# Values' products directly behind k's, scores behind them, and the waits of both at k's last product

## The chip, the core and the metric

The kernel runs on one core of one Trainium2 chip. The core has five engines with a queue of instructions each: TensorE (PE in the profile, with its weight loads shown apart as PEld), VectorE (DVE), ScalarE (ACT), GpSimd (POOL) and SyncE (SP), which here issues the DMAs. Each takes its instructions in the order in which they are written, and they meet at semaphores. The metric is the device time of one execution in microseconds; lower is better.

## What is computed

An input of 128 images with 224 channels and 32 x 32 positions is normalized by groups (16 stripes of two columns), then goes through attention, and is added to the result:

```
xh = group_norm(x)
q, k, v = xh @ Wq, xh @ Wk, xh @ Wv             # 224 -> 224, 8 heads of 28
sim  = q * scale @ k^T + pos_emb                # per head: 16 windows against 16 windows
attn = softmax(sim)                             # for each of 64 places within a window
o    = attn @ v
out  = x + (o @ Wo + bo)
```

The attention is small: each of the 64 places in an 8 x 8 window attends over the same place of the 16 windows, so a score block is 16 x 16 for every head and place.

## The kernel before, in words

An image has 1024 tokens. The work is cut into 512 steps of 256 tokens (two tiles of 128), four steps to an image and two to a half of an image. Every engine runs a function `step(t, i)` for t in order; the middle 480 steps are a loop of 24 steps a round. A step does the stages of different steps of the pipeline: in TensorE's step t the projections belong to u = t + 4, the scores to t + 1, the values' products to t - 2 and the output projection to t - 3.

TensorE's step t, in order (L376 to L424):

- q's product of u (6 matmuls of 512 columns into `ps_q`), v's (12 of 224 columns into `ps_v`), k's (6 of 512 columns into `ps_k`). Before the last of k's six stands `score_waits()` (L379): the scores of t + 1 wait there for `biased` of step t (VectorE has read the scores of step t out of their only buffer, `ps_s`), and in every second step for the block-diagonal keys `k_bd` and for q.
- the scores of t + 1 (`score`, L349): 32 small products of 64 rows and 32 columns, each half of the 128 rows into its own half of `ps_s`; the last raises `scored`.
- three waits, and the values' products of t - 2 (`weigh_values`, L364): 16 small products of 128 rows and 32 columns into `ps_o`; the last raises `pv_done`. They wait for the probabilities `p_bd`, placed by four DMAs, for v in SBUF, and for `o_lo` of t - 3: VectorE has read `ps_o`.
- the output projection of t - 3 into `ps_out` (12 matmuls), behind waits for `o_lo` and `final`; once in four steps a product that totals the squares of an image (`ps_tot`).

The other engines around it:

- ScalarE (step L490) copies q (L501), v (L507), takes the exponential (L511), normalizes x (L484, four instructions a step), copies k into `k_cut` (L518), adds a bias (L470, in two of four steps), and copies the values' result out of `ps_o` into `ohi` (L526). Every second step it also makes `xhi`, the upper 16-bit part of the normalized x (L495). The copy of k waits for `k_done` and for `scored`, because `k_cut` and `k_bd` have two buffers: for even u, the scores asked for are those of t + 1, the ones that TensorE issues right behind this k; for odd u those of t.
- VectorE (step L638) begins with `olo` (L646: what `ohi` lost of `ps_o`), then reads the scores (L651), takes their maximum (L658), transposes the probabilities of the step before (L664), adds the output (L634), and sums (L676).
- GpSimd (step L719) subtracts the maximum (L724), makes `xlo` (L732) in every second step, and multiplies by the reciprocal (L737). The two parts `xhi` and `xlo` are what TensorE's next q product with an even u waits for (L390).

Of the kernel before, what the change touches and what calls it, by code (L numbers as in the profile page):

```python
# [49 lines left out]
PV_LAG, OUT_LAG, FINAL_LAG, STORE_LAG = 2, 3, 4, 7  # L50
# [8 lines left out]
def build(nc, x, wq, wk, wv, wo, bo, pos, scale, out):  # L59
    ctx = ExitStack()  # L60
    with ctx:
# [6 lines left out]
        def sem(name):  # L68
            return ctx.enter_context(nc.semaphore(name))
# [92 lines left out]
        k_done = sem("k_done")  # L162
# [3 lines left out]
        v_kept = sem("v_kept")  # L166
# [11 lines left out]
        pv_done = sem("pv_done")  # L178
        o_hi = sem("o_hi")
        o_lo = sem("o_lo")  # L180
# [7 lines left out]
        def wait(eng, s, n, i, per_round):  # L188

            if isinstance(i, int):  # L190
                if n > 0:
                    eng.wait_ge(s, n)
            else:
                assert n > 0
                eng.wait_ge(s, n + i * per_round)
# [13 lines left out]
        def per_step(eng, s, g, i, each=1):  # L209
            wait(eng, s, each * (g + 1), i, each * PERIOD)  # L210

        def per_half(eng, s, h, i, each=1):
            wait(eng, s, each * (h + 1), i, each * PERIOD // 2)

        def per_image(eng, s, b, i, each=1):
            wait(eng, s, each * (b + 1), i, each * PERIOD // 4)

        def keys_placed(eng, h, i):
            each = 16 * HPG
            wait(eng, k_placed[h % 2], each * (h // 2 + 1), i, each * PERIOD // 4)  # L220

        def probs_placed(eng, g, i):
            each = 16 * PAIRS
            wait(eng, p_placed[g % 2], each * (g // 2 + 1), i, each * PERIOD // 2)

        def image_at(t, lead):
            b, r = divmod(t + lead, 4)
            return b if r == 0 and 0 <= b < B else None
# [5 lines left out]
        def is_step(g):  # L234
            return 0 <= g < STEPS
# [83 lines left out]
        def _(pe):  # L319
            def split_product(dst, w_parts, x_parts, chunks=CH, waits=None):  # L320

                n = 0
                for a, c in PASSES:
                    for ch in range(chunks):
                        if waits is not None and n == 3 * chunks - 1:
                            waits()
                        last = nc.tensor.matmul(dst, w_parts(a, ch), x_parts(c, ch),  # L327
                                                start=(n == 0), stop=(n == 3 * chunks - 1))
                        n += 1
                return last  # L330
# [4 lines left out]
            def project_qk(u, j, waits=None):  # L335
                h, hg = divmod(u, 2)
                c0 = (j * HG + hg) * 128
                return split_product(ps_qk[j][:, :], lambda a, ch: wqk[:, a, ch, c0:c0 + 128],
                                     lambda c, ch: x_parts[c][:, h % 2, ch, :], CH, waits)

            def project_v(g):
                for t2 in range(T2):
                    tok = ((g % 2) * T2 + t2) * TILE
                    last = split_product(ps_v[:, t2, 0:C],
                                         lambda a, ch: x_parts[a][:, (g // 2) % 2, ch, tok:tok + TILE],
                                         lambda c, ch: wv_s[:, c, ch, :])
                return last
# [16 lines left out]
            def weigh_values(g):  # L364
                for t2 in range(T2):
                    for hg in range(HG):
                        for h in range(HPG):
                            unit = (((h // 2) * T2 + t2) * HG + hg) * 2 + h % 2
                            col = (t2 * HG + hg) * 128
                            last = nc.tensor.matmul(  # L370
                                ps_o[h * 32:h * 32 + 32, col:col + 128].rearrange("p (r j) -> p r j", j=32),
                                v_sb[:, g % VBUFS, t2, hg * HPG + h, :],
                                p_bd[:, g % 2, :, unit * 32:unit * 32 + 32], start=True, stop=True)
                return last

            def step(t, i):  # L376
                u = t + PROJ_LEAD

                def score_waits():  # L379
                    g = t + 1  # L380
                    if is_step(g):
                        if g % 2 == 0:
                            keys_placed(pe, g // 2, i)
                            per_step(pe, q_kept, g + 1, i)

                        per_step(pe, biased, g - 1, i)

                if is_step(u):
                    if u % 2 == 0:
                        per_half(pe, x_hi, u // 2, i)  # L390
                        per_half(pe, x_lo, u // 2, i)
                    per_step(pe, q_kept, u - 1, i)
                    project_qk(u, 0).then_inc(q_done, 1)
                    per_step(pe, v_kept, u - 1, i)
                    project_v(u).then_inc(v_done, 1)
                    per_step(pe, k_kept, u - 1, i)
                    project_qk(u, 1, score_waits).then_inc(k_done, 1)
                else:
                    score_waits()
                if is_step(t + 1):  # L400
                    score(t + 1).then_inc(scored, 1)
                g = t - PV_LAG
                if is_step(g):
                    probs_placed(pe, g, i)
                    per_step(pe, v_kept, g, i)

                    per_step(pe, o_lo, g - 1, i)
                    weigh_values(g).then_inc(pv_done, 1)
                g = t - OUT_LAG
                if is_step(g):  # L410
                    per_step(pe, o_lo, g, i)
                    per_step(pe, final, g - 1, i)
                    for ch in range(CH):
                        last = split_product(
                            ps_out[0:CP, ch * 256:ch * 256 + 256].rearrange("p (nh t y) -> p nh t y", nh=NW, t=T2),
                            lambda a, hg: wo_s[:, a, hg, ch * CP:(ch + 1) * CP],
                            lambda c, hg: o_parts[c][:, g % 2, hg::HG].rearrange("p t (nh nw) c -> p nh t (nw c)", nh=NW), HG)
                    last.then_inc(projected, 1)
                b = image_at(t, TOT_LEAD)
                if b is not None:  # L420
                    per_image(pe, joined, b, i)
                    wait(pe, stats, STAT_OPS * (b - 1) + 1, i, STAT_OPS * XBUFS)
                    nc.tensor.matmul(ps_tot[0:CP, :], ones[0:CP, 0:CP], both[:, b % 2],  # L423
                                     start=True, stop=True).then_inc(totals, 1)  # L424
# [342 lines left out]
```

## Time and profile before

| | |
|---|---|
| median of 3 runs | 3675.77 us (3672.93 to 3676.39) |
| the profiled execution's own time | 3674.84 us |
| its span, first to last instruction | 3672.9 us |
| PE busy | 3608.4 us (98% of the span) |
| PEld, DVE, ACT, POOL busy | 71%, 83%, 80%, 56% |
| values' products (L370) and scores (L358), mean of one | 276 ns and 224 ns |
| granted TensorE clock | 1.00 in the whole span (the 2.4 GHz level) |
| PE's share of the chain that ended last | 87% |

PE is the engine that has almost no idle time; the others wait, for each other and for PE. A matmul's end is modelled and overlaps the start of the next, so distances between stages are read from start to start. The profile's rows join equal neighbours ("x2"); the start is that of the first.

### The profile page before, as it was taken

Reading aid. Unit: us, or ns where it says so; the run is one execution under the profiler, and the core shown is the slowest. Engines: PE = TensorE matmul, PEld = TensorE weight load, DVE = VectorE, ACT = ScalarE, POOL = GpSimd, SP = SyncE. Lnnn points to the kernel's source line nnn. Section 1 sums busy time; section 2 is a strip of 40 time slices with the busy share of each in tenths; the row PEclk is TensorE's granted clock in tenths of the full one; section 3 lists DMA queues with packets and bytes.
Section 4 is the critical chain, followed back from the end, with each engine's and each line's share of the span. In section 5 each row is a group of like instructions: output and inputs, shape, how many; then the busy total and the mean of one; then the engine's idle time right before and its main releaser. Section 6 shows DMA issues by size and latency. Waiting matters only on the chain.

```text
span 3672.9 us, 167555 instructions
## 1 busy us (share of the span) xinstructions
PE 3608.4 (98%) x67842; PEld 2625.2 (71%) x67842; DVE 3032.9 (83%) x5028; ACT 2940.0 (80%) x5377; POOL 2045.4 (56%) x3334
## 2 busy tenths in 40 slices
PE   5999999999999999999999999999999999999998
PEld 3777777777777777777777777777777777777776
DVE  6888888888888888888888888888888888888876
ACT  6888888888888888888888888888888888888874
POOL 4555555555555555555555555555555555555553
PEclk9999999999999999999999999999999999999999
DMA  4555555555555555555555555555555555555544
GB/s 95 139 144 136 146 144 142 137 145 143 141 138 150 142 137 143 145 143 137 143 146 144 136 145 144 144 134 145 143 145 135 145 142 145 136 146 143 141 126 117
DMA packets 252111, 513.67 MB, mean 140 GB/s; under 512 B 62672, under 2 KB 63120, under 8 KB 251536
## 3 DMA queue, kind: packets, MB, share of 16 engines
q1 hardware_dynamic: 250000, 504.35, 52.4%
q8 instruction: 554, 9.08, 1.1%
q10 hardware_dynamic: 1536, 0.07, 0.0%
q14 instruction: 21, 0.17, 0.0%
HBM read 118.31 MB, written 117.44 MB: 64 GB/s over the span
## 4 chain that ended last, share of the span: by engine, by line
PE 87%; issue 5%; POOL 3%; DVE 2%; ACT 1%; DMA 0%; POOLq 0%; SPq 0%; DVEq 0%; ACTq 0%
PE ps_out L327 18%; PE ps_q L327 16%; PE ps_k L327 16%; PE ps_v L327 14%; PE ps_o L370 13%; PE ps_s L358 10%; POOL sc L724 1%; ACT xn L484 1%; POOL xlo L732 1%; POOL newton L706 1%; DVE part L622 0%; POOL sc L737 0%; PE ps_tot L423 0%; DVE sc L651 0%; DVE pt_f L664 0%
## 5 line engine op out<-in xcount | busy, mean ns | idle before, releaser
L724 POOL TENSOR_TENSOR sc<-sc,mx 128x512 f32<-128x512 f32 x512 | 536.5, 1048 | 876.3 <-DVE mx L658 876.3
L484 ACT ACTIVATE xn<-x_sb,norm_add,norm_mul 112x128 f32<-112x128 f32 x2048 | 1016.7, 599 | 5.0 <-POOL norm_add L717 3.1
L737 POOL TENSOR_TENSOR sc<-sc,rs 128x512 f32<-128x512 f32 x512 | 536.4, 1048 | 421.7 <-DVE rs L678 421.6
L327 PE MATMUL ps_out<-ohi,wo_s 128*112 128x256 f16 x4096 | 720.8, 278 | 3.1 <-DVE x_sb L634 3.1
L646 DVE TENSOR_TENSOR olo<-ps_o,ohi 128x512 f16<-128x512 f32 x512 | 353.8, 691 | 350.0 <-ACT ohi L526 338.8
L511 ACT ACTIVATE sc<-sc 128x512 f32<-128x512 f32 x512 | 323.3, 632 | 396.3 <-POOL sc L724 396.1
L327 PE MATMUL ps_q<-xhi,wqk 112*128 112x512 f16 x2048 | 611.2, 380 | 12.5 <-POOL xlo L732 9.9
L327 PE MATMUL ps_k<-xhi,wqk 112*128 112x512 f16 x2048 | 609.7, 379 | 0.6 <-ACT q_sb L501 0.6
L370 PE MATMUL ps_o<-p_bd,v_sb 128*32 128x128 f32 x16384 | 553.5, 276 | 9.1 <-DMA p_bd<-pt_f 6.6
L327 PE MATMUL ps_v<-wv_s,xhi 112*128 112x224 f16 x4096 | 560.6, 259 | 0.0
L732 POOL TENSOR_TENSOR xlo<-xn,xhi 112x1024 f16<-112x1024 f32 x256 | 547.3, 2138 | 13.1 <-ACT xhi L495 13.1
L327 PEld LDWEIGHTS ps_out<-ohi,wo_s 128*112 128x112 f16 x4096 | 447.6, 129 | 104.8 <-issue 103.7
L358 PEld LDWEIGHTS ps_s<-k_bd,q_sb 64*32 64x32 f32 x32768 | 360.7, 105 | 218.3 <-issue 215.0
L327 PEld LDWEIGHTS ps_v<-wv_s,xhi 112*128 112x128 f16 x4096 | 395.9, 98 | 121.4 <-issue 0.6
L370 PEld LDWEIGHTS ps_o<-p_bd,v_sb 128*32 128x32 f32 x16384 | 417.3, 109 | 58.4 <-DMA p_bd<-pt_f 7.5
L358 PE MATMUL ps_s<-k_bd,q_sb 64*32 64x64 f32 x32768 | 443.3, 224 | 2.6 <-DVE sc L651 2.6
L501 ACT ACTIVATE q_sb<-ps_q 128x512 f32<-128x512 f32 x512 | 300.4, 587 | 166.0 <-PE ps_q L327 165.0
L327 PE MATMUL ps_out<-olo,wo_s 128*112 128x256 f16 x2048 | 391.1, 273 | 0.0
L651 DVE SCALAR_TENSOR_TENSOR sc<-ps_s,s_scale,pos_sb 128x512 f32<-128x512 f32 x512 | 379.6, 741 | 0.0
L507 ACT ACTIVATE v_sb<-ps_v 128x448 f32<-128x448 f32 x512 | 274.6, 536 | 122.3 <-PE ps_v L327 121.1
L634 DVE SCALAR_TENSOR_TENSOR x_sb<-ps_out,out_scale,x_sb 112x512 f32<-112x512 f32 x512 | 366.5, 716 | 3.3 <-PE ps_out L327 1.7
L327 PE MATMUL ps_v<-wv_s,xlo 112*128 112x224 f16 x2048 | 364.0, 259 | 0.0
(76 smaller groups left out, 5827.6 us busy)
## 6 DMA issues: line engine op xcount, KB each, us to landing
k_bd<-k_cut SPq DMA_DIRECT2D x1024, 128.0 KB
p_bd<-pt_f SPq DMA_DIRECT2D x2048, 64.0 KB, 2.5
x_sb<-in_x SPq DMA_DIRECT2D x256, 448.0 KB, 4.5
out_y<-x_sb SPq DMA_DIRECT2D x256, 448.0 KB, 3.5
k_cut<-in_L_conv_Wq SPq DMA_DIRECT2D x2, 98.0 KB
k_cut<-in_L_conv_Wk SPq DMA_DIRECT2D x2, 98.0 KB
k_cut<-in_L_conv_Wv SPq DMA_DIRECT2D x2, 98.0 KB
pt_f<-in_L_conv_Wo SPq DMA_DIRECT2D x8, 24.5 KB
```

The lines of the kernel that those rows point to most:

```text
L327: last = nc.tensor.matmul(dst, w_parts(a, ch), x_parts(c, ch), start=(n == 0), stop=(n == 3 * chunks - 1))
L358: last = nc.tensor.matmul(ps_s[pr * 32:pr * 32 + 32, half, col:col + 64].rearrange("p (h j) -> p h j", j=32), q_sb[rows, h % QBUFS, hg, to ...
L370: last = nc.tensor.matmul(ps_o[h * 32:h * 32 + 32, col:col + 128].rearrange("p (r j) -> p r j", j=32), v_sb[:, g % VBUFS, t2, hg * HPG + h ...
L484: nc.scalar.activation(xn[:, b % 2, :, c4, :, :, nw].rearrange("p r c q -> p q r c"), x_sb[:, b % XBUFS].rearrange("p ch (nh r w) -> p (ch ...
L501: nc.scalar.activation(q_sb[:, h % QBUFS, hg], ps_qk[0][:, :], ACT.Copy).then_inc(q_kept, 1)
L511: nc.scalar.activation(sc[:, t % 2], sc[:, t % 2], ACT.Exp).then_inc(exped, 1)
L634: nc.vector.scalar_tensor_tensor(xr, ps_out[0:CP, :].rearrange("p (q y) -> p q y", q=CH * NW), out_scale[0:CP, :], xr, ALU.mult, ALU.add). ...
L646: nc.vector.tensor_tensor(olo[:, g % 2], in_x_order(ps_o[:, :]), ohi[:, g % 2], ALU.subtract).then_inc(o_lo, 1)
L651: nc.vector.scalar_tensor_tensor(sc[:, t % 2].rearrange("p (a c) -> p a c", a=2), ps_s[:, :, 0:256], s_scale[:, :], pos_sb[:].rearrange("p ...
L724: nc.gpsimd.tensor_tensor(rows, rows, mx[:, t % 2].unsqueeze(2).broadcast_to(by_row), ALU.subtract).then_inc(shifted, 1)
L732: nc.gpsimd.tensor_tensor(by_channel_half(xlo[:, h % 2]), half_of_xn(h), by_channel_half(xhi[:, h % 2]), ALU.subtract).then_inc(x_lo, 1)
L737: nc.gpsimd.tensor_tensor(rows, rows, rs[:, t % 2].unsqueeze(2).broadcast_to(by_row), ALU.mult).then_inc(probs, 1)
```

## The change

The waits of the values' products go into the same function as those of the scores, ahead of k's last product, and the values' products are issued directly behind k's, with the scores behind them. The scores are cut into halves of 64 rows before as after; `score` and `weigh_values` are the same. No other engine's instructions change.

```diff
-                def score_waits():
+                def attention_waits():
+                    g = t - PV_LAG
+                    if is_step(g):
+                        probs_placed(pe, g, i)
+                        per_step(pe, v_kept, g, i)
+
+                        per_step(pe, o_lo, g - 1, i)
                     g = t + 1
                     if is_step(g):
                         if g % 2 == 0:
...
                     per_step(pe, k_kept, u - 1, i)
-                    project_qk(u, 1, score_waits).then_inc(k_done, 1)
+                    project_qk(u, 1, attention_waits).then_inc(k_done, 1)
                 else:
-                    score_waits()
+                    attention_waits()
+                if is_step(t - PV_LAG):
+                    weigh_values(t - PV_LAG).then_inc(pv_done, 1)
                 if is_step(t + 1):
                     score(t + 1).then_inc(scored, 1)
-                g = t - PV_LAG
-                if is_step(g):
-                    probs_placed(pe, g, i)
-                    per_step(pe, v_kept, g, i)
-
-                    per_step(pe, o_lo, g - 1, i)
-                    weigh_values(g).then_inc(pv_done, 1)
                 g = t - OUT_LAG
```

On PE, in a step of the loop with an even u, before (`ps_s` are the scores, `ps_o` the values' products, `p_placed0` the probabilities, `biased` the read of the scores before):

```order
L327 MATMUL ps_k<-xhi,wqk 128x512
L327 MATMUL ps_k<-xhi,wqk 128x512 [waits biased]
L358 MATMUL ps_s<-k_bd,q_sb 32x64 x32
L195 REGISTER_ALU
L370 MATMUL ps_o<-p_bd,v_sb 32x128 [waits o_lo,v_kept,p_placed0]
L370 MATMUL ps_o<-p_bd,v_sb 32x128 x15
L327 MATMUL ps_out<-ohi,wo_s 112x256 [waits final,o_lo]
```

The same place in the changed kernel:

```order
L327 MATMUL ps_k<-xhi,wqk 128x512
L195 REGISTER_ALU
L327 MATMUL ps_k<-xhi,wqk 128x512 [waits o_lo,biased,v_kept,p_placed0]
L370 MATMUL ps_o<-p_bd,v_sb 32x128 x16
L358 MATMUL ps_s<-k_bd,q_sb 32x64 x32
L327 MATMUL ps_out<-ohi,wo_s 112x256 [waits final,o_lo]
```

The 16 values' products have moved ahead of the 32 scores, and their three waits with the register instruction to k's last product.

On ACT, the end of a step in which the bias is added, and the start of the next; these rows are the same before and after:

```order
L518 ACTIVATE k_cut<-ps_k 128x512 [waits scored,k_done]
L484 ACTIVATE xn<-x_sb,norm_add,norm_mul 112x8x8x2 x2
L195 REGISTER_ALU [waits normed]
L470 ACTIVATE x_sb<-x_sb,bo_sb 112x1024 [waits summed]
L526 ACTIVATE ohi<-ps_o 128x512 [waits projected,pv_done]
L495 ACTIVATE xhi<-xn 112x1024 [waits k_done,normed]
L501 ACTIVATE q_sb<-ps_q 128x512 [waits scored,q_done]
```

Nothing moves here. The `scored` that `k_cut` waits for is raised by the last of the scores, which in the changed kernel stand behind the values' products.

## Rows read from the trace of the kernel before

**Rows 1.** Waits between 100 and 3500 us: engine line <- engine line: us, times, longest
```profile
POOL sc L724 <- DVE mx L658: 817.4, 483, 3.3
DVE olo L646 <- ACT ohi L526: 304.4, 363, 1.2
```
**Rows 2.** One line in that window, DVE L651: instances, min/median/max ns, first and last start
```profile
L651 DVE SCALAR_TENSOR_TENSOR sc<-ps_s,s_scale,pos_sb x483: 740/741/745, 101.3 to 3494.5; 128x512 f32<-128x512 f32 x161
```
**Rows 3.** Timeline of PE, steps A to D: start, us, engine, line, op, count
```profile
3243.25 0.59 PE L327 MATMUL ps_k<-xhi,wqk 112*128 112x512 f16 x2
3243.78 0.86 PE L358 MATMUL ps_s<-k_bd,q_sb 64*32 64x64 f32 x64
3244.57 1.08 PE L370 MATMUL ps_o<-p_bd,v_sb 128*32 128x128 f32 x32
3245.58 0.43 PE L327 MATMUL ps_out<-ohi,wo_s 128*112 128x256 f16 x2
...
3254.05 0.60 PE L327 MATMUL ps_q<-xhi,wqk 112*128 112x512 f16 x2
3254.48 0.59 PE L327 MATMUL ps_q<-xlo,wqk 112*128 112x512 f16 x2
...
3268.10 0.60 PE L327 MATMUL ps_q<-xhi,wqk 112*128 112x512 f16 x2
...
3271.41 0.59 PE L327 MATMUL ps_k<-xhi,wqk 112*128 112x512 f16 x2
```
**Rows 4.** Timeline of ACT in the same stretch
```profile
3244.85 0.66 ACT L518 ACTIVATE k_cut<-ps_k 128x512 f32<-128x512 f32 x1
...
3259.94 0.62 ACT L518 ACTIVATE k_cut<-ps_k 128x512 f32<-128x512 f32 x1
```
**Rows 5.** Timeline of DVE in the same stretch
```profile
3247.83 0.69 DVE L646 TENSOR_TENSOR olo<-ps_o,ohi 128x512 f16<-128x512 f32 x1 [0.28 <-ACT ohi L526]
```
**Rows 6.** Timeline of POOL in the same stretch
```profile
3249.97 1.05 POOL L724 TENSOR_TENSOR sc<-sc,mx 128x512 f32<-128x512 f32 x1 [3.23 <-DVE mx L658]
3250.98 2.14 POOL L732 TENSOR_TENSOR xlo<-xn,xhi 112x1024 f16<-112x1024 f32 x1
...
3265.05 2.14 POOL L732 TENSOR_TENSOR xlo<-xn,xhi 112x1024 f16<-112x1024 f32 x1
```
**Rows 7.** Timeline of all engines near 3626 us, where k_cut waits for the scores
```profile
3625.98 0.86 PE L358 MATMUL ps_s<-k_bd,q_sb 64*32 64x64 f32 x64
...
3626.94 0.60 ACT L518 ACTIVATE k_cut<-ps_k 128x512 f32<-128x512 f32 x1 [1.08 <-PE ps_s L358]
```
**Rows 8.** Timeline near 140 us, where q follows xlo closely
```profile
138.41 2.13 POOL L732 TENSOR_TENSOR xlo<-xn,xhi 112x1024 f16<-112x1024 f32 x1
...
140.46 0.38 PE L327 MATMUL ps_out<-ohi,wo_s 128*112 128x256 f16 x2
...
140.77 0.60 PE L327 MATMUL ps_q<-xhi,wqk 112*128 112x512 f16 x2
```
**Rows 9.** Timeline of another such stretch, 228 to 257 us
```profile
228.42 0.59 PE L327 MATMUL ps_k<-xhi,wqk 112*128 112x512 f16 x2
...
230.64 0.63 ACT L518 ACTIVATE k_cut<-ps_k 128x512 f32<-128x512 f32 x1
...
250.78 2.13 POOL L732 TENSOR_TENSOR xlo<-xn,xhi 112x1024 f16<-112x1024 f32 x1
...
253.19 0.60 PE L327 MATMUL ps_q<-xhi,wqk 112*128 112x512 f16 x2
...
256.50 0.59 PE L327 MATMUL ps_k<-xhi,wqk 112*128 112x512 f16 x2
```
**Rows 10.** What the values' products (L370) waited for, whole span: us, times
```profile
issue: 6.9, 31
```
**Rows 11.** SP's timeline after 3249 us, and p_bd's DMAs: KB each, median us to landing
```profile
3250.63 2.43 SPq L302 DMA_DIRECT2D p_bd<-pt_f  x4
...
p_bd<-pt_f SPq DMA_DIRECT2D x1932, 64.0 KB, 2.5
```

## The prediction

> **What bounds the kernel now.** I read the page's busy times first. PE is busy in 98% of the span and 87% of the last chain is PE, so it sets the time. Then the waits: POOL waits 817 us for VectorE's maximum, VectorE 304 us for ACT's `ohi`, in a window of 3400 us [rows 1]; ACT's exponential in turn takes what POOL made. So the softmax engines are not full, but each waits for the next of them: they form a ring, and a delay put into it anywhere goes round. A step takes (3494.5 - 101.3) / 482 = 7.04 us, four steps 28.16 us [rows 2]. The pattern repeats every four steps; I call them A to D, A being the one that ends with `ps_tot`. I look at one such stretch from 3243 us on [rows 3 to 6], and at one near 228 us. In the second, PE needs 256.50 - 228.42 = 28.08 us for four steps [rows 9]: I take that for PE running freely; the mean is 0.08 us over it.
>
> **PE's own part: nothing.** From the start of k's last pair to the scores it takes 0.53 us, from the scores' start to the values' 0.79, from the values' to the output projection 1.01, together 2.33 us [rows 3]. In the new order the same pieces stand as 0.53 (k's pair), 1.01 (values), 0.79 (scores), again 2.33. I take it that a distance belongs to the product in front: its streaming and the emptying of the array behind it. What the change of neighbours could do is bounded by the rows too. A pair of 512-column products takes 0.43 us where the next is of its kind (3254.05 to 3254.48), and 0.53 before the scores: the emptying costs 0.10. So 0.10 us a step is what a cheaper neighbour could give, and as much I allow for a dearer one. I take zero, since the values and the output projection both use 128 rows and their distance is not shorter for it.
>
> The Trainium skill (TensorEngine Tiling (Array Packing), Key Properties) says that changing the tiling mode drains TensorE. There are three changes of mode in a step before and three after, so by that rule the sum is zero as well; if only a change of the row split drained, the step would lose one drain, 0.10 us. The row from the values to the output projection speaks for the rule.
>
> **The waits that move.** The values' three waits and their register instruction stand between scores and values now, and cost PE 6.9 us in 31 places in the whole run [rows 10]. Behind k's fifth product they are covered by the products still queued there. None comes later than the wait for `biased`, which is there already: `olo` of that step ends at 3247.83 + 0.69 = 3248.52, and VectorE writes it just before it reads the scores. The probabilities' four DMAs are issued from 3250.63 to 3253.06 and land some 2.5 us later, at about 3255.6 [rows 11]; the values that need them follow the k of the next step, step C's at 3257.36. That leaves 1.8 us. In front of the output projection stand two waits, `o_lo` and `final`, now behind the scores; the values' own three, which stood there, fit into that distance in all but those 31 places. So the gain is at most 6.9 us, and only if PE sets the time everywhere.
>
> **What the later scores do.** This is the term that decides. The scores now start at 3243.25 + 0.53 + 1.01 = 3244.79 and end 0.86 later at 3245.65, where before they ended at 3244.64 [rows 3]. Their users:
>
> - VectorE's read of them (L651) stands behind `olo`, which ends at 3248.52 [rows 5], 2.9 us after the new end; no cost.
> - `k_cut` of an even u asks for just these scores. Where it waited for them, it started 3626.94 - (3625.98 + 0.86) = 0.10 us behind their end [rows 7]. So in step A it can start at 3245.75 at the earliest. It starts at 3244.85 now [rows 4]: it is held 0.90 us. In step C it starts at 3259.94 [rows 4]; k's last pair began at 3254.05 + 3.31 = 3257.36 (the 3.31 is worked out below), so it is 2.58 us behind k already, and the new bound is 2.50: no new wait; B and D ask for scores of the step before.
>
> Behind `k_cut` in ACT's queue stand normalization, bias and `ohi`, and nothing of it can pass. The Trainium skill says the same of ScalarE's queue (TensorE: Matmul & The Clock Gate, the table at its head: a strict FIFO of 8); by a queue that let `ohi` pass, the whole term below would be zero.
>
> From there I follow the ring in the rows: `k_cut` 3244.85 [rows 4], `olo` 3247.83, waiting for `ohi` [rows 5], the maximum, then POOL's L724 at 3249.97 after 3.23 us of idleness for the maximum, and `xlo` right behind it, 3250.98 to 3253.12 [rows 6]. Nobody in this chain has a pause in which 0.90 us could vanish: VectorE waits for ACT, POOL for VectorE, `xlo` stands behind POOL's L724. So `xlo` ends at 3254.02. PE's q of step C starts at 3254.05 [rows 3]. The slack of 0.93 us is used up.
>
> How close may q follow `xlo`? Near 140 us, `xlo` ended at 140.54 and q started at 140.77, 0.23 us behind, and 0.31 after the last pair of the output projection instead of 0.22 (the pace of such pairs): there the wait was felt [rows 8]. In the code the semaphore wait, a register instruction with the second wait, and a third wait on q's first product follow each other. So q of C moves to 3254.25, by 0.20.
>
> The delay goes on in the ring: `k_cut` of C follows that of A by 15.09 us (3259.94), the next `xlo` starts at 3265.05 and ends at 3267.19 [rows 6], 22.34 us after A's `k_cut`. With the 0.90 it ends at 3268.09, and q, at 3268.10 before [rows 3], starts 0.23 later at 3268.32. Again 0.22 late, the first 0.20 included. Then A comes again, and again `k_cut` waits for the scores: the ring is tied to PE there, and PE to the ring at q, so the delay repeats every four steps.
>
> The new cycle, from k's last pair in A to the next: 0.53 + 1.01 + 0.86 + 0.10 = 2.50 to `k_cut`; 22.34 to the end of `xlo`; 0.23 to q; 3271.41 - 3268.10 = 3.31 to k's last pair: 28.38 us. In the stretch of rows 9, where the ring already runs later relative to PE, the middle is 250.78 + 2.13 - 230.64 = 22.27 and the cycle 2.50 + 22.27 + 0.23 + 3.31 = 28.31. I take their mean, 28.34. Against 28.16 that is 0.18 us per four steps; 483 steps are 120.75 cycles [rows 2], so +21.7 us. The ends of the run I leave out. The 6.9 us do not come back, as PE waits for `xlo` anyway.
>
> 3674.84 + 21.7 = 3696.6 us by the profiled execution. Its time is 0.9 us under the median of the runs, so I say 3697.
>
> **Bounds.** The 0.23 could be as short as the handing over of 0.10 that `k_cut` showed: the cycle is then 28.21 and the loss 6 us, 3681. At the other end, the full 28.38 and no relief: +0.22 x 120.75 = 27 us, 3702, and some us more where the probabilities, whose slack falls from 1.8 to 0.9 us, come late in a step with more DMAs.
>
> **Rivals.**
>
> 1. The ring has cover. Somewhere the 0.90 us is caught (a wait that I took for a link is slack) and `xlo` stays ahead of q. Then only the waits' gain is left, 6.9 us or less: 3668 to 3676. For it: 0.93 us of slack at q is just as much as the hold of 0.90, and PE before has a slack everywhere. Against: q needs 0.23 us more than the bare end of `xlo`. Chance 0.10, half of it inside 0.2%.
> 2. Cheaper changes of mode: k's products and the values' both use all rows, so the values start without a drain, 0.10 us x 512 steps = 51 us: 3624. Against: the same pair of row splits stands between values and output projection now and is no shorter. 0.03.
> 3. The wait for the probabilities decides, now ahead of k's last product. The place is k of step C, with B's probabilities; it binds from 1.8 us of added delay on [rows 11], and earlier where DMAs of x and of the output stand in front in SP's queue. The ring's 0.9 brings it half way. If it cost 0.20 us, as the wait at q does, once in four steps on top, that is 128 x 0.20 = 26 us: 3723. Chance 0.06.
> 4. The ring is held, but q can follow closely: loss 3 to 8 us, 3678 to 3683. 0.10, a third of it inside 0.2%.
>
> My forecast has 0.71. About 0.2% (7 us) is what a measurement of this kernel tells from no change. Slower: 0.71 + 0.06 + 0.07 = 0.84. Same: 0.05 + 0.03 = 0.08. Faster: 0.05 + 0.03 = 0.08. The range reaches from 3678 to 3708.
>
> **What would show it.** In the profile after: PE's distances k to values 0.53, values to scores 1.01, scores to output 0.79; ACT's `k_cut` waiting for `ps_s` about 120 times, some 0.6 to 0.9 us each, where the waits before have no such row; `q` starting about 0.23 us behind the end of `xlo`, with an idle of PE before it put down to POOL L732, about 240 times; the slack of `biased` at k's last product down to a few tenths. I am wrong if q of steps A and C still follows the output projection at 0.22 us, or if `k_cut` shows no wait for the scores.

## The result, and the profile after

The changed kernel takes 3719.29 us (median of 6 runs, 3709.58 to 3723.88), the kernel before 3675.31 us beside it (6 runs, 3672.93 to 3676.39): ratio 1.0117, 95% interval 1.0105 to 1.0129, a loss of 44 us. I had forecast a loss of 22, with 3708 as the high end. The direction and its mechanism came out as forecast; the size did not. The profiled execution of the kernel after took 3719.29 us, with a span of 3717.5.

The page's head of the kernel after, with the busy times:

```profile
span 3717.5 us, 167883 instructions
PE 3641.3 (98%) x67842; PEld 2614.5 (70%) x67842; DVE 3033.2 (82%) x5028; ACT 2924.8 (79%) x5377; POOL 2044.2 (55%) x3334
```

PE's busy time grew by 33 us with the same products (short waits vanish under the modelled ends, and products at the lower clock count longer), so the page's shares tell nothing here. DVE and POOL worked as long as before, ACT 15 us less. The waits between 100 and 3500 us, as in [rows 1]: engine and line that waited, what for, us, times, longest:

```profile
POOL sc L725 <- DVE mx L659: 842.6, 477, 5.1
ACT sc L512 <- POOL sc L725: 506.3, 469, 1.4
DVE olo L647 <- ACT ohi L527: 396.7, 382, 1.7
...
PEld ps_q L327 <- issue: 35.9, 149, 0.6
PEld ps_k L327 <- issue: 23.8, 96, 0.4
PEld ps_out L327 <- issue: 12.4, 22, 2.6
ACT k_cut L519 <- PE ps_s L358: 10.5, 31, 1.3
PE ps_out L327 <- issue: 8.5, 5, 2.4
```

Two rows of the kernel before, for comparison:

```profile
ACT sc L511 <- POOL sc L724: 364.8, 483, 1.4
...
PEld ps_q L327 <- issue: 2.1, 5, 0.6
```

Three things to see. The ring waits longer at every link: VectorE for `ohi` 397 us instead of 304, ACT for POOL 506 instead of 365. The weight loads of q wait 149 times, about 0.24 us each; before, 5 times. And there is a row that nothing in my forecast spoke of: PE standing in front of the output projection, 5 times, up to 2.4 us.

One cycle of four steps in the kernel after, the rows that answer to [rows 3, 4, 6]. Timeline of PE, ACT and POOL: start, us, engine, line, what:

```profile
3223.62 0.59 PE L327 MATMUL ps_k<-xhi,wqk 112*128 112x512 f16 x2
3224.14 1.08 PE L370 MATMUL ps_o<-p_bd,v_sb 128*32 128x128 f32 x32
3225.15 0.91 PE L358 MATMUL ps_s<-k_bd,q_sb 64*32 64x64 f32 x64
3225.99 0.43 PE L327 MATMUL ps_out<-ohi,wo_s 128*112 128x256 f16 x2
...
3226.09 0.60 ACT L519 ACTIVATE k_cut<-ps_k 128x512 f32<-128x512 f32 x1 [0.26 <-PE ps_s L358]
...
3232.17 2.12 POOL L733 TENSOR_TENSOR xlo<-xn,xhi 112x1024 f16<-112x1024 f32 x1
...
3234.53 0.60 PE L327 MATMUL ps_q<-xhi,wqk 112*128 112x512 f16 x2
...
3246.20 2.13 POOL L733 TENSOR_TENSOR xlo<-xn,xhi 112x1024 f16<-112x1024 f32 x1
...
3248.57 0.60 PE L327 MATMUL ps_q<-xhi,wqk 112*128 112x512 f16 x2
...
3251.88 0.59 PE L327 MATMUL ps_k<-xhi,wqk 112*128 112x512 f16 x2
```

k to values 0.52, values to scores 1.01, scores to output projection 0.84 (0.79 in most steps). `k_cut` begins 2.47 us behind k's last pair (2.50 forecast). From `k_cut` to the end of the next `xlo` it takes 3234.29 - 3226.09 = 8.20 us (8.27 in the rows before), and q starts 0.24 us behind the end of `xlo` in both places. The cycle is 3251.88 - 3223.62 = 28.26 us (28.34 forecast). This one is among the short ones: over the 119 cycles from one `ps_tot` to the next in the 480 steps counted below, the median is 28.34 us (28.14 before), just the forecast; the mean is 28.48 us (28.18 before), and what lies between median and mean is the unforeseen part.

The unforeseen part, in the kernel after. Timeline of PE near 1410 us; the figure in brackets is PE's idle time before the row and what ended it, "issue" being nothing that the profile shows:

```profile
1409.20 1.08 PE L370 MATMUL ps_o<-p_bd,v_sb 128*32 128x128 f32 x32
1410.21 0.86 PE L358 MATMUL ps_s<-k_bd,q_sb 64*32 64x64 f32 x64
1413.09 0.43 PE L327 MATMUL ps_out<-ohi,wo_s 128*112 128x256 f16 x2 [2.02 <-issue]
...
1414.46 1.06 PE L327 MATMUL ps_q<-xhi,wqk 112*128 112x512 f16 x2
```

And its stretches: us of the stretch, busy times, granted clock, DMA share:

```profile
1410.00:1414.00 4.00, 1.98 (x84) 1.62 (x76) 2.77 (x6) 3.43 (x8) 3.45 (x12) 1.00 0.38 102
1414.00:1418.00 4.00, 4.00 (x19) 2.19 (x17) 3.97 (x6) 1.50 (x3) 2.38 (x4) 0.57 0.15 35
```

PE stands still for 2.0 us, though what it waits for by the program (`o_lo`, `final`) is long there, and then works some 3.4 us at the 1.2 GHz level: the pair of q takes 1.06 instead of 0.60 us. One such event costs some 2.0 + 1.7 = 3.7 us.

### The profile page after: what moved, and what is told of

Read it like the earlier page. It is cut to its first block, busy times and chain, and to the rows that moved or that the text cites. A ratio compares the mean times of both kernels' runs of the same rounds, so it can differ in the third digit from the quotient of the medians.

```text
span 3717.5 us, 167883 instructions
## 1 busy us (share of the span) xinstructions
PE 3641.3 (98%) x67842; PEld 2614.5 (70%) x67842; DVE 3033.2 (82%) x5028; ACT 2924.8 (79%) x5377; POOL 2044.2 (55%) x3334
## 4 chain that ended last, share of the span: by engine, by line
PE 96%; issue 2%; DVE 1%; ACT 1%; SPq 0%; DMA 0%; POOL 0%; ACTq 0%; POOLq 0%; DVEq 0%
PE ps_out L327 20%; PE ps_q L327 18%; PE ps_k L327 17%; PE ps_v L327 16%; PE ps_o L370 14%; PE ps_s L358 11%; PE ps_tot L424 0%; DMA p_bd<-pt_f 0%; SPq L302 0%; ACT xn L485 0%; SPq L310 0%; DMA x_sb<-in_x 0%; DVE sc L652 0%; POOL xlo L733 0%; DVE pt_f L665 0%
## 5 line engine op out<-in xcount | busy, mean ns | idle before, releaser
L370 PEld LDWEIGHTS ps_o<-p_bd,v_sb 128*32 128x32 f32 x16384 | 417.1, 110 | 212.0 <-issue 201.5
L370 PE MATMUL ps_o<-p_bd,v_sb 128*32 128x128 f32 x16384 | 555.2, 276 | 9.2 <-DMA p_bd<-pt_f 9.1
L659 DVE TENSOR_REDUCE mx<-sc 128x16 f32<-128x512 f32 x512 | 351.3, 686 | 13.2
```

What stands on the lines that cost most here:

```text
L370: last = nc.tensor.matmul(ps_o[h * 32:h * 32 + 32, col:col + 128].rearrange("p (r j) -> p r j", j=32), v_sb[:, g % VBUFS, t2, hg * HPG + h ...
L659: nc.vector.reduce_max(mx[:, t % 2], rows, axis=AX.X).then_inc(maxed, 1)
```

## The experiments

Sixteen kernels were run. Each is told with the ratio to the kernel before on the same chip. For the accounting I took from each trace the same 480 steps, from k's last product of step 16 to that of step 496, and three sums: what the distance from the output projection to q is over its usual 0.11 us, without stalls; the distances over 1 us between two products of PE ("stalls"); and the stretches at the 1.2 GHz level between 100 and 3500 us, each of which costs about half its length.

```
kernel                               time us   480 steps   at q     stalls       at 1.2 GHz
before                               3675      3381.0       1.7      0    -         0    -
after                                3719      3418.3      27.3      5   10.2       3   10.2
e1  after, k_cut without `scored`    3671      3379.9       0.1      1    1.4       0    -
e2  before, the same                 3673      3379.1       1.1      0    -         0    -
e3  new order only                   3739      3437.3      30.4     20   32.6       0    -
e4  moved waits only                 3680      3383.5       1.6      5    8.8       0    -
e5  e3, k_cut without `scored`       3673      3378.4       0.8      0    -         0    -
e6  new order in steps A only        3732      3433.1      25.6     14   25.3       4   13.7
e7  new order in B, C, D only        3674      3378.1       0.6      1    1.8       0    -
e9  after, bias behind ohi           3670      3376.8       0.0      1    1.3       0    -
e8  e1 and e9 together               3673      3381.1       0.1      1    1.1       0    -
e11 before, bias behind ohi          3669      3377.5       0.1      0    -         0    -
e13 before, 128 waits at the head    3733      3434.7       0.1     19   47.7       7   23.9
e12 e5, the same                     3749      3456.4       0.1     20   58.4      13   44.4
e14 after, the same                  3814      3517.5      22.4     35   88.2      17   64.8
e10 e3, the same                     3830      3533.4      22.1     46  106.2      16   61.4
e15 after, 64 waits at the head      3811      3507.8      21.6     24   72.9      17   78.5
e16 after, 192 waits at the head     3779      3483.6      19.3     22   54.9      13   51.2
```

### Is it the wait of k_cut? (e1, e2)

e1 is the changed kernel, e2 the kernel before, both with this one line less (for even u it asks for the scores just issued):

```diff
                     per_step(act, k_done, u, i)
-                    per_step(act, scored, 2 * (h - 2) + 1, i)
```

> The changed kernel, but ScalarE's copy of k (k_cut) no longer waits for the scores; the buffer is still safe, since SyncE issues the DMAs out of k_cut only behind VectorE's transpose, which stands behind those scores. Theory H (the hold of k_cut by the later scores, carried round the ring of ScalarE, VectorE and GpSimd into xlo and from there into PE's q): k_cut in step A starts where it did before, 1.4 to 2.0 us behind k's last product, xlo is ahead of q again by 0.5 to 1 us, PE runs at 28.1 us per four steps, and the time is that of before or under it: 3660 to 3678. Theory W (PE's own order costs: the stalls of about 2 us in front of the output projection and the waits gathered at k's last product): the loss stays, 3705 to 3725, with xlo early. If H explains the regular part and the rare stalls are of the order itself, the time is 3678 to 3690 and the stalls in front of the output projection are still in the profile.

> The kernel before without the wait of k_cut for the scores, as a control for the run above. Before, k_cut waited for the scores hardly anywhere, so H and W both expect no change: 3670 to 3680. Were it faster by over 8 us, the wait itself (the two semaphores on one ScalarE instruction) would cost something, and the run above would have to be read against this one.

Measured: e1 3671.48 us (11 runs), ratio 0.9991 [0.9982, 1.0]; e2 3672.58, 0.9996 [0.9986, 1.0005]; both within what theory H expected. The whole 44 us is gone from the changed kernel with one wait of ACT, and the same wait is worth nothing in the kernel before. The order of the products therefore has no price of its own on PE, and in this pair, whose PE programs are the same, the stalls (1 instead of 5) and the slow stretches (none instead of 3) hang on the hold too.

### Which half of the change? (e3, e4)

e3 has the new order with the values' waits directly in front of the values (the diff is against the kernel before, where these lines stand behind the scores). e4 is the changed kernel with the two lines of the scores back in front of the two of the values: the moved waits and the old order.

```diff
+                if is_step(t - PV_LAG):                 # e3
+                    probs_placed(pe, t - PV_LAG, i)
+                    per_step(pe, v_kept, t - PV_LAG, i)
+                    per_step(pe, o_lo, t - PV_LAG - 1, i)
+                    weigh_values(t - PV_LAG).then_inc(pv_done, 1)
                 if is_step(t + 1):
                     score(t + 1).then_inc(scored, 1)
```

> Only the order of the change: values' products behind k and in front of the scores, but their three waits directly in front of them and not at k's last product. H expects what the changed kernel does, 3705 to 3725, with q 0.236 us behind xlo in steps A and C. W expects that the waits gathered at k's last product make up a good part of the loss, and so 3680 to 3700 here.

> Only the waits of the change: the values' three waits stand at k's last product, but the scores still come in front of the values' products. H expects no loss and at most the 6.9 us of issue gaps back: 3667 to 3677. W expects a loss of 10 us or more.

Measured: e3 3739.44 us, 1.0181 [1.0166, 1.0197]; e4 3680.46 us, 1.0018 [1.0009, 1.0027]. Theory H missed both: e3 is slower than its 3705 to 3725 us, e4 than its 3667 to 3677. So the order is what costs, and with it the moved waits help by 20 us; alone they cost 6. In e4 the gain that I had forecast did come: the distances from the scores to the values sum up to 70.1 us over the 480 steps, where the kernel before has 75.8. Five stalls of 8.8 us in all ate it. The waits of e3 between 100 and 3500 us:

```profile
PE ps_out L327 <- issue: 26.4, 19, 2.2
...
PE ps_q L327 <- issue: 6.9, 19, 0.7
```

In e3 a stall comes every 172 us, in 19 of the loop's 20 rounds, in front of the same output projection of the loop's body. In e4 four stand at that place and one at the loop's end, with no more loss at q than before, though 85 q products start within 0.4 us of the end of `xlo` (11 before, 221 in the changed kernel).

### Ring free, order kept (e5)

```diff
                     per_step(act, k_done, u, i)                   # in e3
-                    per_step(act, scored, 2 * (h - 2) + 1, i)
```

> The values' and scores' products in the new order, the values' waits directly in front of the values, and ACT's k_cut without its wait for the scores (a race-free cut here, since the scores that it waited for are read by VectorE before xlo can be reached). The run with the new order and the same places of the waits, but with k_cut's wait, took 3739 us and showed 19 stalls of 1.3 to 2.5 us on PE in front of or inside the output projection, once a round of the loop. Theory F (the stalls come when PE's sequencer has been let go late and has no lead over the engine; the held ring makes it late): the q waits go and the stalls mostly with them, 3672 to 3685 us, fewer than 8 rows of PE idle over 1 us in front of the output projection. Rival L (the stalls hang on where the instructions lie, whatever the ring does): only the q waits go (31 us of the 64), the 19 stalls stay, 3700 to 3712 us.

Measured: 3672.84 us, 0.9994 [0.9985, 1.0004], as theory F expected. All of e3's 64 us are gone. The row of its waits:

```profile
PE ps_out L327 <- issue: 0.6, 1, 0.6
```

The 19 stalls have gone with the hold of the ring, though PE's own program is the same, word for word. At this point I took the lateness of PE's sequencer (the part of PE that passes the waits and issues the instructions) for the whole cause of the stalls; the padded kernels below add a second sort.

### Which step? (e6, e7)

```diff
-                if is_step(t - PV_LAG):
+                values_first = t % 4 == 0       # e6; e7 has t % 4 != 0
+                if values_first and is_step(t - PV_LAG):
                     weigh_values(t - PV_LAG).then_inc(pv_done, 1)
                 if is_step(t + 1):
                     score(t + 1).then_inc(scored, 1)
+                if not values_first and is_step(t - PV_LAG):
+                    weigh_values(t - PV_LAG).then_inc(pv_done, 1)
```

> The changed kernel with the new order (values, then scores) only in the steps that I call A (every fourth), where k_cut asks for the scores just made; in the three others scores stand first again. All waits at k's last product. Theory H (the loss is the hold of k_cut in step A, carried round the ring): the loss stays whole, q about 0.24 us behind xlo in A and C, 3697 to 3720 us. Rival (the loss is made in every step, by the later scores or by the order of the modes): a quarter of 44 us, 3685 us or less.

> The complement: the new order in steps B, C and D, scores first in A. All waits at k's last product. Theory H: k_cut in A starts as early as in the kernel before (about 1.4 us behind k's last product began) and the loss is that of the moved waits alone, 3672 to 3684 us. Rival (the loss is made in every step): three quarters of 44 us, about 3708 us.

Measured: e6 3731.61 us, 1.016 [1.0133, 1.0187], above the 3720 us that theory H allowed; e7 3674.20 us, 0.9996 [0.9986, 1.0005], as it expected. The new order in one step of four makes the whole loss at q (25.6 us against 27.3); in the three others it makes none. e6 even came out 12 us above the changed kernel, all of it in stalls (14 against 5) and slow stretches: another arrangement of the same code, another number of stalls.

### Hold kept, ring shortened (e9)

```diff
-                add_bias(image_at(t, SPLIT_LEAD - 1), 0, i)
-                add_bias(image_at(t, SPLIT_LEAD - 2), 1, i)
...
                     nc.scalar.activation(ohi[:, g % 2], in_x_order(ps_o[:, :]), ACT.Copy).then_inc(o_hi, 1)
+                add_bias(image_at(t, SPLIT_LEAD - 1), 0, i)
+                add_bias(image_at(t, SPLIT_LEAD - 2), 1, i)
```

> The changed kernel with ACT's two add_bias moved from in front of ohi to behind it in the step, so that the ring from k_cut to xlo becomes about 1.0 us shorter in the step with the bias while k_cut is still held by the scores. Theory H (the loss is ring length, not the hold as such): k_cut of step A still starts 2.28 us behind k's last product, but xlo ends early enough again that q follows the output projection at its own pace; 3665 to 3682 us. Rival (the hold or the order costs PE by itself, or bias is late now and k's last product waits for it): 3700 us or more.

Measured: 3670.37 us, 0.9986 [0.9976, 0.9996]. Its waits between 100 and 3500 us:

```profile
DVE olo L647 <- ACT ohi L525: 294.8, 195, 2.6
...
ACT k_cut L519 <- PE ps_s L358: 179.9, 241, 1.1
ACT q_sb L502 <- PE ps_q L327: 179.5, 241, 1.4
```

`k_cut` is now held 241 times, 0.75 us each, 180 us in all: far more than in the changed kernel (31 times), and it costs nothing. This is the clearest of the runs: the hold is not the loss. The loss at q is a ring whose length, together with the hold, exceeds PE's four steps; with 1.1 us of bias out of its way it fits again. The Trainium skill (TensorE: Matmul & The Clock Gate, the table at its head) gives ScalarE's queue as strictly first in, first out. The trace agrees: `ohi` came earlier when it was put earlier in the queue, and VectorE waited 295 us for it instead of 397.

### A better kernel? (e8, e11)

e8 is e1 and e9 in one; e11 is the kernel before with only the bias moved.

> The changed kernel without k_cut's wait for the scores, and with ACT's add_bias behind ohi: both cuts of the ring at once, looked at as a candidate. Theory H (PE sets the time alone once the ring is free): like the two single cuts, 3665 to 3674 us, since PE's own 28.08 us per four steps, found in the stretch near 228 us, is the floor; no mid-run stretch at the 1.2 GHz level. Rival (the ring still costs something in the single cuts): 3660 us or less.

> The kernel before, with nothing changed but ACT's add_bias behind ohi. Theory H: the kernel before lost 0.08 us per four steps to the ring; without that 10 us less at most, 3665 to 3673 us. Rival (the gain of this edit needs the new order): 3673 us or more.

Measured, 11 runs each: e8 3673.09 us, 0.9995 [0.9986, 1.0004]; e11 3669.02 us, 0.9985 [0.9976, 0.9994]. Two cuts of the ring are no better than one: once the ring fits, PE alone sets the time. e11 is the fastest version found, by 0.15% (some 6 us), level with e9. The 1.7 us at q are gone, and its 480 steps take 3.5 us less; the new order adds nothing to it. The 28.08 us per four steps that the prediction took for PE running freely are its best case and not its mean: the cycles of e1, e2, e5, e7, e8, e9 and e11 average 28.13 to 28.17 us, against 28.18 in the kernel before. So the ring cost the kernel before a few microseconds at most, and not 0.08 us a cycle.

### Where the code lies (e10, e12 to e16)

The trace has a queue of the kind "instruction" (q8) with 554 transfers in the whole run, of about 1.1 us each; that they bring PE's instructions is borne out below, where more waits on PE alone make them more. At each of the four longest stalls of the changed kernel and of e3 (2.2 to 2.6 us from product to product), such a transfer begins between 0.12 us before and 0.35 us after the start of the last product in front of the stall. It holds for every stall of the table: in front of each of the 214 products that end one, the last transfer had ended 1.2 to 2.1 us before. A transfer comes every 6.6 us, so by chance this would be so for about one in seven. So I put more instructions at the head of PE's program, outside the loop, which moves the loop's code against the pieces in which it is delivered:

```diff
             pe.wait_ge(zeroed, N_ZEROED)
+            for _ in range(128):
+                pe.wait_ge(zeroed, N_ZEROED)
             rounds(pe, step, before_11=bound_weights, before_4=weights_split)
```

> The run with the new order and the values' waits directly in front of the values (3739 us, 19 stalls over 1.3 us of PE in front of the output projection, once a round of the loop at one place), with 128 more waits on a semaphore that has long been raised at the head of PE's program, outside the loop: the loop's instructions lie elsewhere. Theory F (the stalls are late deliveries of PE's instructions, which the trace shows as transfers of about 1 us): the stalls change their place or their number, the q waits (31 us) stay; 3705 to 3740 us. Rival S (the stalls are a late semaphore of another engine at that place of the schedule): they stay where they are, 19 of them, 3739 us within 4 us. If the loop's code keeps its place against the borders of the deliveries, F too would leave them there, and the run would not tell.

Measured: 3829.65 us, 1.0419 [1.0403, 1.0435], far above theory F's 3705 to 3740. 128 waits that are passed at once, outside the loop, cost 90 us. The page of e10, queue, packets, MB, share:

```profile
q8 instruction: 572, 9.37, 1.1%
```

18 more deliveries than the 554 of the kernels without padding, about one for each of the loop's 20 rounds. A late semaphore of another engine at one place of the schedule as the cause (rival S, 3739 us) is out.

> The new order with k_cut's wait taken away (3673 us), with the same 128 waits at the head of PE's program that took the version with the wait from 3739 to 3830 us. Theory F (a late delivery of instructions costs PE only where its sequencer has been let go late): the ring is free, so 3670 to 3690 us and few stalls over 1 us. Rival L (with this layout the deliveries are late whatever the ring does): about 90 us more than without the padding, 3740 us or more.

> The kernel before with the same 128 waits at the head of PE's program. Theory F: its q waits are passed with 0.5 to 1.0 us to spare, so some stalls at most: 3672 to 3700 us. Rival L: 90 us more, 3750 us or more. If it came out between, the lead of PE's sequencer in the kernel before would be just about what a delivery takes.

> The changed kernel with the same 128 waits. Theory F: its q waits (27 us) stay, and the stalls (12 us in the run, with their stretches at 1.2 GHz) come out in another number and at other places, as they did in the version with the values' waits directly in front of them: 3740 to 3830 us. If the place of the values' waits decides, the stalls stay few and the time within 15 us of 3719.

Measured: e12 3749.40 us, 1.0207 [1.019, 1.0224]; e13 3733.28, 1.016 [1.0143, 1.0176]; e14 3813.79, 1.0382 [1.036, 1.0404]. Here my theory F missed: with a free ring (3690 us at most) the padding still costs 77 us, and the kernel before (3700 at most) loses 59. Rival L's 3740 us or more was met by e12, its 3750 or more was not by e13; for the changed kernel F's 3740 to 3830 held. A stall of e13, timeline of PE:

```profile
310.06 0.38 PE L327 MATMUL ps_out<-ohi,wo_s 128*112 128x256 f16 x2
313.23 0.60 PE L327 MATMUL ps_q<-xhi,wqk 112*128 112x512 f16 x2 [2.79 <-issue]
...
314.53 0.94 PE L327 MATMUL ps_v<-wv_s,xhi 112*128 112x224 f16 x4
```

and its wait's row, between 100 and 3500 us:

```profile
PE ps_q L327 <- issue: 42.5, 19, 2.9
```

Again once a round, and again with slow stretches behind some of them (7). But the place is another one than in e3, and it tells what the padding did: the stall stands at the return of the loop, between a round's last output projection and the next round's first q. PE's branch instruction at the end of the round stands at 308.7 us in the trace, its next entry of the sequencer at 312.8. In the kernels without padding these two are 0.4 to 1.8 us apart, in the padded ones 2.8 to 4.6, with one delivery more in between. Sorted by place, the stalls of the 480 steps are ("the loop's end" is behind the last round):

```
                                  at the loop's return   elsewhere
before, e2, e5, e11               0                      0
e1                                0                      1
e7, e8, e9 (each)                 1 (the loop's end)     0
e4                                1 (the loop's end)     4    7.3 us
after                             1 (the loop's end)     4    8.7
e6                                1 (the loop's end)     13   23.5
e3                                1                      19   31.6
e13  padded, ring not held        19   47.7 us           0
e12  padded, ring free            19   56.5              1    1.8
e16  padded, held                 19   51.2              3    3.6
e15  padded, held                 19   67.1              5    5.8
e14  padded, held                 19   57.7              16   30.4
e10  padded, held                 19   63.4              27   42.8
```

> The changed kernel with 64 more waits at the head of PE's program. The q waits (25 to 28 us over the kernel before) stay by every theory, since they need no delivery. If the stalls are a matter of where the loop's code lies, they come out otherwise than in the changed kernel (12 us) and than with 128 waits (about 100 us): anything from 3700 us (none left) to 3830 us. If only the ring's hold made them, 3719 us within 8.

> The same with 192 waits. By the layout: again another number between 3700 and 3830 us, unlike the one with 64 waits by more than 10 us; 3700 us would mean that the ring's part of the loss is 25 us and the rest is layout. By the hold alone: 3719 us within 8.

Measured: e15 3810.70 us, 1.0376 [1.0358, 1.0393]; e16 3779.00 us, 1.0277 [1.026, 1.0294]. By the layout, 3700 to 3830 us and over 10 us apart was expected, and that is what came; the hold alone (3719) is out. The loss at q is 19 to 22 us in every padded version with the hold; the stalls are 24 of 73 us and 22 of 55 us, 19 of them at the loop's return in either. None of the three paddings is without this stall, so 3700 us, the changed kernel with the ring's loss alone, was not reached.

What follows for the stalls: there are two sorts. The one at the loop's return comes with the padding, once a round, in every padded version and whatever the ring does; with the slow stretches behind it, it is nearly all that padding cost the two versions without a hold. The other sort, within the body, is the one that the changed kernel has. For it theory F still stands. Versions that lose nothing to a late `xlo` have 0 or 1 of them, padded or not; versions with the hold and the long ring have 3 to 27. The same body code has 4, 5, 16 and 3 of them with 0, 64, 128 and 192 waits in front (the changed kernel, e15, e14, e16), so the place of the code counts there too. e4 has 4 without a hold; its q products often follow `xlo` closely, as told above, which fits but was not tested by itself. That the sequencer is let go too late to hide a delivery is the reading that fits all this; no row shows it directly. I did not settle why a product starts 1.2 to 2.1 us after its delivery has ended, nor when an idle gap is followed by a slow stretch: the three of 2.02 to 2.43 us in the changed kernel were, the longest of e3 (2.2 us) and 12 of the 19 at e13's loop return were not.

## Why the prediction was wrong in size and right in kind

- **PE's own part: nothing.** Right. The pieces are the same ones in another order, and e1, e5 and e7 (new order, 0.9991, 0.9994, 0.9996) show no price of it. The sums over the 480 steps say the same of each piece: from k to what follows 148.3 us before and 148.4 in e5, from the values to what follows 97.2 in both, from the scores to what follows 70.1 in e4 (old order, waits moved) and 70.2 in e5. The Trainium skill (TensorEngine Tiling (Array Packing), Key Properties) says that a change of tiling mode drains the array. With three changes in either order it gave zero too, and these sums agree; they do not show a drain as such. A drain less, worth 51 us, is excluded.
- **The waits that move: at most 6.9 us back.** The distance itself gave back 5.7 us in e4. The time did not: e4 is 6 us slower, since stalls of 8.8 us come with it, for which the forecast had no term; nor did it see that under the new order the moved waits leave fewer stalls (e3 to after, 20 us).
- **The hold of `k_cut` in step A, carried round the ring.** Right: 2.47 us behind k's last pair, q 0.24 us behind `xlo`, in A and C; e6 and e7 show that step A alone does it, e1 and e9 that it is the ring. The size: 27.3 us at q against 1.7 before, so 25.6 where I had 21.7, within its bounds of 6 and 27. As a cycle, the median is 28.34 us as forecast. (By its own terms the sum of the forecast is 3696.5 and not 3696.6 us, which changes nothing.)
- **What would show it.** The sign at `k_cut` came out otherwise: 31 waits, not 120, a third of a microsecond each. The waits of q are there, but under "issue" at the weight loads, 149 times, and not under POOL L732 about 240 times; counted by distance, 221 q products start within 0.4 us of the end of `xlo`. With the ring late, ACT arrives at `k_cut` only just before the scores end, because its idleness has moved to the exponential, waiting for POOL (506 us against 365). Where ACT is early (e9), the hold shows in full. Rivals 1 and 4 (cover; q follows closely) are out, 2 too; rival 3 (the probabilities) shows 0.2 us once between 100 and 3500 us. It came closest in time (3723) by chance.
- **The step that failed** is the sum and its high end: "At the other end, the full 28.38 and no relief: ... 3702, and some us more", together with "The ends of the run I leave out". It took the loss at q for the only thing that a late ring can do to PE, and so put stalls, slow stretches and ends at nothing. The sum that the trace after gives: 25.6 us at q; 4 stalls in front of the output projection and one at the loop's end, 10.2 us of which some 9 are over the usual distance; three stretches at 1.2 GHz of 3.41 us, half of it 5; other distances 2 to 3 us less; together the 37.3 us of the 480 steps (3418.3 - 3381.0). The remaining 7 us lie in the ends: 2.5 in front of the 480 steps and 4.8 behind. The granted clock shows four slow stretches there (at 52.5, 3687.7, 3697.9 and, cut off by the end, 3715.0 us) against one before (at 3670.2, cut off too), a full one worth 1.7 us, and the last probabilities are waited for 9.1 us instead of 6.6 (row of the kernel after, 3500 us to the end). How these share the 7 us is not shown; e5 and e7 have slow stretches near their end too, without a loss.

```profile
PE ps_o L370 <- DMA p_bd<-pt_f: 9.1, 3, 5.4
```

So the loss at q, 25.6 of 44 us, is the part that was forecast. The stalls in the body hang on the hold in the two pairs that differ in it alone (e1 against the changed kernel, e5 against e3), while e4 has four without it; that an instruction delivered late makes them rests on the 214 transfers and on the padding.

- Could the profile before have told of the stalls? No: its 480 steps have none. A wider high end, for a PE whose slack of 0.93 us in front of q the forecast itself used up, would have been the right answer. Once the kernel had run, the spread of its runs (14 us, against 3.5 before) said that something irregular was in them.

## What to carry to other kernels

Look for rings: engines that each wait for the next have a period, and a wait that is moved back by 0.9 us costs only what the ring's period then exceeds the bound engine's; shorten the ring anywhere (here one instruction behind another) and the wait is free. When instructions are reordered on an engine, ask what other engines' waits its semaphores release, since the price is paid there. And where the engine that sets the time runs a long loop body and a change makes its waits pass late, leave room in the range for late instructions. Distrust differences of one or two per cent between two versions whose code lies differently: padding the program's head shows how much hangs on that, but look at where its stalls stand, since at the loop's return they say nothing on the body.

## What the runs showed of the hardware

- 64 to 192 instructions in front of a loop made a kernel slower by 59 us (before; 54 of them in the 480 steps of the loop's middle, 3434.7 - 3381.0), 60 to 95 us (after), 77 and 90 us (e12, e10). The body of the loop was the same.
- In all of these, one stall a round (19 in the 480 steps, 2.5 to 3.5 us each in the mean) stood at the loop's return, where one more delivery of instructions fell.
- The stalls took PE 1.0 to 4.6 us from product to product; the deliveries of instructions in the traces take 1.1 to 1.2 us (0.9 to 2.5). The product that ends a stall started 1.2 to 2.1 us behind the end of a delivery, 214 times of 214.
- Before each of the three mid-run stretches at the 1.2 GHz level in the changed kernel PE had been idle for 2.02 to 2.43 us. They lasted 3.41 us; in e14, of 17 such stretches, two lasted 6.83. The kernels whose stalls were all under 2 us or absent had none in mid-run.
- q started 0.24 us behind the end of the `xlo` that it waited for, in hundreds of places; `k_cut`, where held, 0.04 to 0.28 us behind the end of the scores (median 0.10 in e9, 242 places).
